# Layer 1's layer norm in one loop over the chunks, its reciprocal roots by Ln and Exp on ScalarE and a Newton step on VectorE

## The reference

```
x = x + _L1(_gn(x))            # _gn: group norm, 32 groups of 6 channels
def _L1(x):                    # for each image, n = 4096 positions, c = 192
    xf  = x.reshape(b, c, h*w).transpose(0, 2, 1)
    mu  = mean(xf, axis=-1);  var = mean((xf - mu)**2, axis=-1)
    xn  = (xf - mu) * rsqrt(var + 1e-5) * ln_w + ln_b
    Q, K, V = xn @ Wq.T, xn @ Wk.T, xn @ Wv.T
    S   = Q @ K.T                                # 4096 x 4096
    attn = a1 * softmax(S) + a2 * relu(S)**2     # a1, a2 from w1, w2
    return (attn @ V).transpose(0, 2, 1) + x
```

## Time and profile before

| | us |
|---|---|
| median of 3 runs | 3456.6 |
| the profiled execution | 3457.51 |
| its span, first to last instruction | 3455.7 |
| TensorE busy in it | 3209.4 (93%) |
| ScalarE busy | 2149.9 (62%) |
| VectorE busy | 1903.4 (55%) |
| GpSimd busy | 994.5 (29%) |
| mean granted TensorE clock | 0.967 of full |

### The profile page before, as it was taken

One profiled execution on the slowest core, in us unless ns is written; L12 is line 12 of the kernel. 1 busy time (PEld: TensorE's weight loads), 2 busy tenths in 40 slices (PEclk: granted clock), 3 DMA queues, 4 the chain that ended last, 5 costly groups with the idle time before them and its releaser, 6 DMA issues. The chain is left out here.

```text
span 3455.7 us, 48136 instructions
## 1 busy us (share of the span) xinstructions
PE 3209.4 (93%) x16482; PEld 1290.6 (37%) x16482; DVE 1903.4 (55%) x2454; ACT 2149.9 (62%) x2363; POOL 994.5 (29%) x507
## 2 busy tenths in 40 slices
PE   3799999999999999999999768999999668999998
PEld 1222322223223222232222224555555324555554
DVE  6451347521563425455210155888888546888886
ACT  5256556565555665565666403988888126888886
POOL 2002021020030200210200021666666233666665
PEclk8799999999999999999999888999999789999999
DMA  5312112121132111310200233777777534777777
GB/s 142 91 33 61 45 39 66 44 44 49 33 82 52 25 44 43 74 49 10 63 8 8 54 88 95 132 144 143 144 143 140 123 96 99 143 143 144 142 142 133
DMA packets 688680, 289.44 MB, mean 84 GB/s; under 512 B 603218, under 2 KB 644946, under 8 KB 686482
## 3 DMA queue, kind: packets, MB, share of 16 engines
q1 hardware_dynamic: 688500, 287.16, 38.9%
HBM read 89.17 MB, written 34.28 MB: 36 GB/s over the span
## 5 line engine op out<-in xcount | busy, mean ns | idle before, releaser
L435 ACT ACTIVATE prob<-ps_s,cur 128x1024 f32<-128x1024 f32 x1024 | 1084.5, 1109 | 721.3 <-PE ps_s L635 719.7
L648 PE MATMUL ps_a<-prob,vt 128*64 128x512 f32 x4096 | 992.8, 605 | 0.0
L1307 POOL TENSOR_TENSOR p_lo<-gp,p_hi 128x1024 f16<-128x1024 f32 x256 | 551.9, 2166 | 403.1 <-ACT p_hi L1406 398.0
L1534 PE MATMUL ps_s<-kst,qs 128*128 128x512 f16 x2560 | 639.4, 383 | 19.9 <-DMA qs<-q_scratch 11.7
L1547 PE MATMUL ps_o<-v_hl,at_hi 128*128 128x384 f16 x2048 | 549.3, 329 | 29.5 <-DMA at_lo<-p_lo 29.1
L629 PE MATMUL ps_s<-q_a,k_a 128*128 128x512 f16 x2048 | 533.2, 382 | 13.7 <-DMA q_b<-lo 9.0
L1547 PE MATMUL ps_o<-v_hl,at_lo 128*128 128x192 f16 x2048 | 505.9, 248 | 0.0
L648 PEld LDWEIGHTS ps_a<-prob,vt 128*64 128x64 f32 x4096 | 248.6, 136 | 409.8 <-issue 408.2
L1781 DVE TENSOR_SCALAR_CACHE_REDUCE neg<-ps_s,mix 128x1024 f32<-128x1024 f32 x256 | 327.4, 1279 | 128.6 <-PE ps_s L1534 127.1
L1534 PEld LDWEIGHTS ps_s<-kst,qs 128*128 128x128 f16 x2560 | 244.8, 99 | 246.9 <-issue 22.9
L629 PEld LDWEIGHTS ps_s<-q_a,k_a 128*128 128x128 f16 x2048 | 137.6, 97 | 522.6 <-ACT prob L435 437.3
(11 more groups left out here) (214 smaller groups left out, 2752.6 us busy)
## 6 DMA issues: line engine op xcount, KB each, us to landing
z<-z_scratch SPq DMA_DIRECT2D x80, 384.0 KB, 3.7
sq<-rn_scratch SPq DMA_DIRECT2D x14, 768.0 KB, 10.1
qs<-q_scratch SPq DMA_DIRECT2D x64, 128.0 KB, 2.8
q_a<-hi SPq DMA_DIRECT2D x64, 96.0 KB, 2.3
rden<-den_scratch SPq DMA_DIRECT2D x64, 96.0 KB, 2.1
o_scratch<-o_s SPq DMA_DIRECT2D x64, 96.0 KB, 2.0
o_buf<-o_scratch SPq DMA_DIRECT2D x16, 384.0 KB, 4.2
x_buf<-in_x SPq DMA_DIRECT2D x16, 384.0 KB, 5.1
```

The lines of the kernel that those rows point to most:

```text
L435: act.activation(prob[:, a % PR, :], ps_s[:, a % 2, :], ACT.Exp, bias=cur[:, slot:slot + 1], scale=1.0 / SPLIT).then_inc(exped, 1)
L648: ins = pe.matmul(ps_a[h * HALF:(h + 1) * HALF, j % 2, :], vt[:, slot, m, :], prob[:, a % PR, h * CH:(h + 1) * CH], start=(m == 0), stop=( ...
L1307: pool.tensor_tensor(p_lo[:, cols], prob[s][:, cols], p_hi[:, cols], ALU.subtract).then_inc(lo_made[c], 1)
L1534: ins = pe.matmul(ps_s[:, c % 2, h * CH:(h + 1) * CH], qs[:, s, qt, :], kst[:, ktile, cols], start=(t == 0), stop=(t == len(terms) - 1))
```

## The change

The three loops and the stage between them become one loop with one to three chunks of offset between its steps. In step i TensorE does the mean of chunk i, the variance of chunk i-1 and q and V of chunk i-2. The means and variances go to the two halves of `ps_o`, which the preparation otherwise leaves free by then, and no longer through the pair in `ps_s`. ScalarE does, in this order: the V copy of chunk i-3, the square of chunk i, Ln and Exp for the root of chunk i-1, the q copy of chunk i-2, the bias (two Identity operations in place of L1763) and the float16 copy of chunk i-1. VectorE: the low part of V of chunk i-3, the deviation of chunk i, three operations of a Newton step and the two scalings of chunk i-1, the low part of q of chunk i-2. The root is exp(-0.5 ln(2 var + 2e-5)); the factor of the square root of two and a sign are put into the weight once. All 96 partitions hold every variance, so nothing crosses partitions and the four small DMAs, GpSimd's power and the copies to `vb` are gone. `fit_weights` moves to between the deviations of chunks 0 and 1. The group-norm scaling is done in two halves of 2048 columns. `below_xs` is a tile that is not used: it moves `xs` off the memory of `xg`, which is still being read.

```diff
-        PRO = 8 * 3 + 16
+        PRO = NCH + 2 * NCH
...
+        eps2 = sb("eps2", [CP, 1])
...
+            below_xs = sb("below_xs", [CP, CT, 2 * CH], F32, second)
...
-                    sp.wait_ge(s_free, b * PRO + 2 + 24)
-                    sp.dma_start(m_dram, vb[0:1, :]).then_inc(v_out, 16)
-                    sp.wait_ge(v_out, 16 * b + 16)
-                    sp.dma_start(tv[:, :], m_dram.rearrange("o (p t) -> (o p) t", p=P)).then_inc(v_in, 16)
-                    sp.wait_ge(tok, TOK * b + 4)
-                    sp.dma_start(r_dram.rearrange("o (p t) -> (o p) t", p=P), ty[:, :]).then_inc(r_out, 16)
-                    sp.wait_ge(r_out, 16 * b + 16)
-                    sp.dma_start(rn[0:CP, :], r_dram.partition_broadcast(CP)).then_inc(r_in, 16)
-
                     sp.wait_ge(res_out, 16 * NCH * (b + 1))
...
+                pool.memset(eps2[:, :], 2e-5)
...
-                    pool.wait_ge(g_made, CT * b + CT)
                     for c in range(NCH):
+                        pool.wait_ge(g_made, 2 * CT * b + CT * (1 + c // 4))
                         cols = slice(c * CH, (c + 1) * CH)
                         pool.tensor_tensor(xg[:, :, cols], xg[:, :, cols], g[:, :, cols], ALU.add).then_inc(xg_made, 1)
-                    pool.wait_ge(pow_asked, 2 * b + 3)
-                    pool.tensor_tensor(ty[:, :], tv[:, :], mhalf[:, :], ALU.pow).then_inc(powed, 1)
...
-                    for c in range(NCH):
+                    def square_dev(c):
...
+                            act.wait_ge(var_full, NCH * b + c - 1)
                         act.activation(sq_buf[:, c % 2, :, :], g[:, :, c * CH:(c + 1) * CH], ACT.Square).then_inc(sq_made, 1)
 
+                    def first_root(c):
+
+                        cols = slice(c * CH, (c + 1) * CH)
+                        act.wait_ge(var_full, NCH * b + c + 1)
+                        act.activation(rn[0:CP, cols], ps_o[0:CP, CH:2 * CH], ACT.Ln, bias=eps2[:, 0:1],
+                                       scale=2.0).then_inc(root_made, 1)
+                        act.wait_ge(root_made, 2 * (NCH * b + c) + 1)
+                        act.activation(rn[0:CP, cols], rn[0:CP, cols], ACT.Exp, scale=-0.5).then_inc(root_made, 1)
+
                     def high_x(c):
-                        act.wait_ge(ln_op, LN * b + 4 * c + 4)
+                        cols = slice(c * CH, (c + 1) * CH)
+                        for t in range(CT):
+                            act.wait_ge(ln_op, CT * (NCH * b + c) + t + 1)
+                            act.activation(g[:, t, cols], g[:, t, cols], ACT.Identity, bias=pvec[:, t, 2:3]).then_inc(x_done, 1)
+                        act.wait_ge(x_done, CT * (NCH * b + c) + CT)
                         if c >= 2:
                             act.wait_ge(k_in[c % 2], 6 * 16 * (NCH // 2 * b + c // 2))
-                        act.activation(xs[:, c % 2, 0, :, :], g[:, :, c * CH:(c + 1) * CH], ACT.Copy).then_inc(xh_made, 1)
-
-                    def high_qv(c):
-                        u = 24 + 2 * c
+                        act.activation(xs[:, c % 2, 0, :, :], g[:, :, cols], ACT.Copy).then_inc(xh_made, 1)
+
+                    def high_q(c):
+                        u = NCH + 2 * c
                         act.wait_ge(s_full, b * USE + u + 1)
                         if c >= 2:
                             act.wait_ge(q_out[c % 2], 4 * 16 * (NCH // 2 * b + c // 2))
                         act.activation(qst[:, c % 2, 0, :, :], ps_s[0:CP, u % 2, :].rearrange("p (t n) -> p t n", t=CT),
                                        ACT.Copy).then_inc(ph_made, 1)
-                        u += 1
+
+                    def high_v(c):
+                        u = NCH + 2 * c + 1
                         act.wait_ge(s_full, b * USE + u + 1)
                         act.activation(v_hl[:, 4 * c:4 * c + 4, 0:C], ps_s[:, u % 2, :].rearrange("p (m d) -> p m d", m=4)[:, :, 0:C],
                                        ACT.Copy).then_inc(ph_made, 1)
 
-                    for c in range(NCH):
-                        high_x(c)
-                        if c >= 2:
-                            high_qv(c - 2)
-                    high_qv(NCH - 2)
-                    high_qv(NCH - 1)
+                    for i in range(NCH + 3):
+                        if i >= 3:
+                            high_v(i - 3)
+                        if i < NCH:
+                            square_dev(i)
+                        if 1 <= i <= NCH:
+                            first_root(i - 1)
+                        if 2 <= i <= NCH + 1:
+                            high_q(i - 2)
+                        if 1 <= i <= NCH:
+                            high_x(i - 1)
...
+                    def mean_of(c):
+                        pe.wait_ge(g_made, 2 * CT * b + CT * (1 + c // 4))
+                        if c:
+                            pe.wait_ge(dev_made, NCH * b + c)
...
-                            ins = pe.matmul(ps_s[0:CP, i, 0:CH], meanm[:, :], g[:, t, c * CH:(c + 1) * CH],
+                            ins = pe.matmul(ps_o[0:CP, 0:CH], meanm[:, :], g[:, t, c * CH:(c + 1) * CH],
...
-
-                    for c in range(NCH):
+                        ins.then_inc(mean_full, 1)
+
+                    def variance_of(c):
                         pe.wait_ge(sq_made, NCH * b + c + 1)
...
+                        if c:
+                            pe.wait_ge(root_op, 3 * (NCH * b + c - 1) + 1)
...
+                            ins = pe.matmul(ps_o[0:CP, CH:2 * CH], meanm[:, :], sq_buf[:, c % 2, t, :],
...
+                        ins.then_inc(var_full, 1)
+
+                    def q_and_v(c):
+                        pe.wait_ge(x_done, CT * (NCH * b + c) + CT)
...
+                    for i in range(NCH + 2):
+                        if i < NCH:
+                            mean_of(i)
+                        if 1 <= i <= NCH:
+                            variance_of(i - 1)
+                        if i == 2:
+                            pe.wait_ge(wqk_set, 1)
+                        if i >= 2:
+                            q_and_v(i - 2)
...
+                    dve.tensor_scalar(pvec[:, :, 1:2], pvec[:, :, 1:2], -(2.0 ** 0.5), None, ALU.mult)
...
-                    for t in range(CT):
-                        dve.tensor_scalar(g[:, t, :], xg[:, t, :], gst[:, 0, t:t + 1], gst[:, 3, t:t + 1],
-                                          ALU.subtract, ALU.mult).then_inc(g_made, 1)
-                    dve.wait_ge(g_made, CT * b + CT)
-
-                    for c in range(NCH):
+                    for h in range(2):
+                        cols = slice(h * N // 2, (h + 1) * N // 2)
+                        for t in range(CT):
+                            dve.tensor_scalar(g[:, t, cols], xg[:, t, cols], gst[:, 0, t:t + 1], gst[:, 3, t:t + 1],
+                                              ALU.subtract, ALU.mult).then_inc(g_made, 1)
+
+                    def deviate(c):
                         cols = slice(c * CH, (c + 1) * CH)
-                        i = full()
+                        dve.wait_ge(mean_full, NCH * b + c + 1)
+                        dve.wait_ge(g_made, 2 * CT * b + CT * (1 + c // 4))
                         dve.wait_ge(xg_made, NCH * b + c + 1)
                         for t in range(CT):
-                            ins = dve.tensor_tensor(g[:, t, cols], g[:, t, cols], ps_s[0:CP, i, 0:CH], ALU.subtract)
+                            ins = dve.tensor_tensor(g[:, t, cols], g[:, t, cols], ps_o[0:CP, 0:CH], ALU.subtract)
                         ins.then_inc(dev_made, 1)
+
+                    def second_root(c):
+
+                        cols = slice(c * CH, (c + 1) * CH)
+                        at = 3 * (NCH * b + c)
+                        dve.wait_ge(root_made, 2 * (NCH * b + c) + 2)
+                        dve.scalar_tensor_tensor(out=vb[0:CP, cols], in0=ps_o[0:CP, CH:2 * CH], scalar=1e-5, in1=rn[0:CP, cols],
+                                                 op0=ALU.add, op1=ALU.mult).then_inc(root_op, 1)
+                        dve.wait_ge(root_op, at + 1)
+                        dve.tensor_tensor(vb[0:CP, cols], vb[0:CP, cols], rn[0:CP, cols], ALU.mult).then_inc(root_op, 1)
+                        dve.wait_ge(root_op, at + 2)
+                        dve.scalar_tensor_tensor(out=rn[0:CP, cols], in0=vb[0:CP, cols], scalar=-1.5, in1=rn[0:CP, cols],
+                                                 op0=ALU.add, op1=ALU.mult).then_inc(root_op, 1)
+                        dve.wait_ge(root_op, at + 3)
+
...
-                        dve.sem_inc(s_free, 1)
-                    for c in range(NCH):
-                        i = full()
-                        dve.tensor_copy(vb[0:CP, c * CH:(c + 1) * CH], ps_s[0:CP, i, 0:CH]).then_inc(s_free, 1)
-
-                    if not b:
-                        fit_weights()
-                    dve.wait_ge(v_in, 16 * b + 16)
...
```

(85 more changed lines are left out.)

14 lines of the change are left out of this document (1 added, 13 removed).

## The result

The changed kernel takes 3475.8 us (median of five runs, 3473.8 to 3475.9) against 3456.6: 1.0055 of the time before, 95% interval 1.0044 to 1.0066. The profiled execution took 3473.9 us, span 3472.1, granted clock 0.965 (0.967 before). It is slower by 19 us, where 21 were forecast.

The account below looks back on a forecast made before the run. Bound: the two images' preparations, remade into a serial ScalarE-VectorE relay. Start, steps and tail gave image 1 133.5 us (6.5 more) and image 0 142.3 (14.4 more): 3457.5 + 20.9 = 3478 us, 8-in-10 range 3450 to 3493.

Parts of the forecast that it names:

- Bound and place: Each image's preparation, first group-norm scaling to first score matmul: 127.87 and 126.98 us, together 254.85 of 3455.7.
- Part 1, loads: Ln and Exp on ScalarE: two table loads a chunk, 32 of 1.28 us, 41 us of ScalarE.
- Part 2, ring: Serial relay between ScalarE and VectorE from one xs copy to the next: 13.4 us a chunk, at most 14.3.
- Second ring: Through SP's K and q stores, q copy waiting for stores of two chunks back: 11.4 us, under 13.4.
- Rival 1: One table serves Ln and Exp in each chunk: steps mostly 11.4 us, total 3449; chance 0.12.
- Part 3, starts: GpSimd's adds block VectorE at each image's start: first xs copy after 36.6 us (image 0), 27.8 (image 1).
- rival 2: GpSimd's adds don't block VectorE: starts 24.0 and 19.8 us, total 3458, no change; chance 0.14.
- Part 4: Seven steps to the last xs copy, 89.3 us, the last 12.0; then a tail of 16.4 us.
- Rest: Row loops and their Exp table unchanged, time there within +-2 us.
- Rival 3: Loads cost more than their row (3520), or TensorE stays at the half clock (3515); chance 0.08.

Follow-up runs that it names:

- x1: Changed kernel with one table set loaded by name for all of layer 1, in place of 32 loads: 3444.3 us, 0.9971 of before.
- x3: Changed kernel, table loads kept, with deviation (VectorE) and square (ScalarE) written ahead of V's low part and V copy: 3461.1 us, 1.0017 of before.
- x8: Changed kernel with the one table, and SP issuing the q stores before the K stores: 3426.8 us, 0.9922 of before.
- x2: Changed kernel with GpSimd's eight adds per image cut from 512 to 32 columns, a probe only: 3458.7 us, 1.0012 of before.
- x6: Changed kernel with one table, deviation and square ahead of V parts, and q stores before K stores on SP: 3412.8 us, 0.9886 of before.
- x7: x6 with fit_weights moved ahead of the group-norm scaling: 3417.6 us, 0.9894 of before.

## Why the prediction was right

**Bound and place.** Right. All of the loss lies between the scaling and the first score of the two images: +19.6 of the forecast +20.9.

**Part 1, loads.** 32 of 1.28 us without a pause round them, as taken. x1 puts their whole price at 29.4 us in the preparations (31.5 between the medians); the rule that one load would do was true of the hardware and not of this kernel.

**Part 2, ring.** 13.4 forecast, 13.43 measured. Ln and Exp took 0.68 and 0.63, where 0.68 and 0.60 were taken from an Identity. x3 shows that V's low part was a member of it, and that the swap gives 1.43 and not the 2.3 expected, since q's low part, which the prediction had inside the ring, was next, and V's copy stayed a member between Square and Ln.

**Second ring.** 11.4 forecast, 11.2 in x1. Rival 1 was worked out to 7.8, 10.9, then 11.4 apart, 119.9 us for image 1 and 3449; x1 has 7.6 (image 0), 10.7, 11.2, 119.8 and 3444.3. That the q stores were its reason is shown by x8.

**Part 3, starts.** Sizes right (36.6 for 36.4, 27.8 for 27.5), one reason incomplete. In image 0 deviation 1 ended 25.9 us in, for 26.1. In image 1 two errors of about 2 us cancel. The prediction had the mean at TensorE's full speed and deviation 1 ending at 11.6; it ended at 13.5. TensorE's first mean product of the changed kernel, and a window over it:

```profile
2018.68 3.73 PE L1502 MATMUL ps_o<-gp,meanm 96*96 96x512 f32 x4 [4.38 <-DVE gp L1732]
```

```profile
2018.00:2028.00 10.00, 7.23 (x9) 2.20 (x10) 9.90 (x12) 1.06 (x1) 9.30 (x4) 0.50 0.27 79
```

The granted clock is 0.50, the 1.2 GHz level. Against that, only two VectorE steps of chunk 0 were stretched, by 3.5 us together, not four: the adds were over by then. So rival 2, which had 3458, came to its time in x2 (3458.7) with starts of 25.1 and 23.4 where 24.0 and 19.8 were forecast. Its two preparations are 4.0 us longer than that rival had them (259.2 for 255.2), and the stretch between them 3.0 shorter: the agreement of the sum is luck. x2 also spares the scaling 2.0 us (5.12 for 7.14), which the prediction had not counted.

**Part 4.** The steps came to 88.7 and 88.8 us for 89.3, the tail to 16.8 and 16.4 for 16.4. The last step was 11.2, not 12.0.

**Rest.** "Within 2" was 3.2: the time outside the two preparations fell by 3.2 us, 2.8 of it between them. All eleven kernels with the new loop have this stretch at 609.0 to 611.2 us, against 613.2 in the one trace of the kernel before; no run isolates the reason. The forecast of 3478.5 before rounding is 4.6 above the profiled 3473.9: 3.2 for this, 1.4 in the preparations.

**Rival 3.** No load drained the engine. The half clock did come, but while the ring is a relay it costs only the starts: q at lower speed fits in TensorE's pauses. From 2076 to 2106 the clock was 0.85 and a q product took 5.34 us, from 2800 to 2860 it was 1.00, and in both the copies were 13.43 apart. The rival's sum was also wrong: 14 steps of 4 us on 3478 are 3534, not 3515. The 6.5 and 10.0 us a chunk of TensorE were too high (6.03 and 9.47 in x6), without effect here, as TensorE wasn't in the ring.

## What to carry to other kernels

A loop over engines that each run in order costs the sum of its longest relay, as long as that is more than the busiest engine's work (13.43 against 9.47 us here): write the relay down, with every piece that stands between two of its members on their queues, and after each piece removed look for the one that was hidden behind it. Two functions that share a table set cost one load if that set is loaded by name, and cost two a turn here, where it was left to the placement. Here the change lost 0.55% as made and won 1.6% with four edits: the table, two orders, and a residual that reads one tile.

## What the runs showed of the hardware that was not expected

- GpSimd's add held up more VectorE operations than those with two SBUF inputs. A tensor_scalar of one SBUF tile of 96 x 2 (L1671) took 2.19 us beside it, against 0.17 in x2 and x7. Those of 128 x 1 (L1662, L1664) took 0.13 to 0.15. The Trainium skill has tensor_scalar among the operations that can use the shared port ("SBUF — State Buffer", Who interferes with whom); the trace agrees for 96 x 2.
- The group-norm scaling, in four pieces of 2048 columns beside the adds, took 7.14 us; the two of 4096 before the adds took 4.73, and in x2 the four took 5.12.
- On GpSimd a multiply-add with one SBUF tile, 96 x 512, took 14.12 / 16 = 0.88 us; an add of two tiles, 96 x 1024, 20.54 / 8 = 2.57 with VectorE's turns between (2.31 in the earlier trace rows).
